# Eight dense layers on node features: a unit of two node chunks, one in each half of the partitions

## What is computed

```python
def _mlp1(x, W, b):
    return jax.nn.silu(x @ W + b)
def _res(h, W1, b1, W2, b2):
    return h + _mlp1(_mlp1(h, W1, b1), W2, b2)
res_h = nodes
h = _mlp1(nodes, Wh, bh)
h = _propagate(h, edge_attr, edge_index, We, be, Wl)
h = _res(h, r1_W1, r1_b1, r1_W2, r1_b2)
h = _mlp1(h, Wm, bm)
h = h + res_h
h = _res(h, r2_W1, r2_b1, r2_W2, r2_b2)
h = _res(h, r3_W1, r3_b1, r3_W2, r3_b2)
h = _propagate(h, edge_attr, edge_index, We, be, Wl)
```

## Time and profile before

| | us |
|---|---|
| median of 3 runs | 13832.53 |
| lowest and highest of them | 13831.42, 13838.11 |
| the profiled execution | 13845.22 |
| its span, first to last instruction | 13843.5 |

### The profile page before, as it was taken

How to read it: one execution, slowest core, us unless ns; L and a number is a source line. 1 busy time by engine, 2 the same in 40 slices (tenths; PEclk the granted TensorE clock), 3 DMA queues, 4 the chain that set the end, 5 groups by cost and what they waited for, 6 DMA issues and landing times.

```text
span 13843.5 us, 199525 instructions
## 1 busy us (share of the span) xinstructions
PE 9124.3 (66%) x43992; PEld 6407.8 (46%) x43993; DVE 7459.0 (54%) x18791; ACT 3827.0 (28%) x8556; POOL 9553.0 (69%) x8478
## 2 busy tenths in 40 slices
PE   0266665776663679897666666766666656667676
PEld 0011112222111345554666666466666655666666
DVE  8876665777761220101343333333343348999998
ACT  0144445444410111111222222222222222333332
POOL 0168887888886766564777777467777757777774
PEclk9999999999996779898555555555555555665665
DMA  9942222222226999799644444244444438999996
GB/s 380 406 90 19 20 19 14 20 20 20 20 14 216 379 354 324 278 325 219 110 106 104 103 103 104 54 97 104 104 105 104 104 82 171 178 177 177 177 179 128
DMA packets 1476698, 1975.29 MB, mean 143 GB/s; under 512 B 1005691, under 2 KB 1023803, under 8 KB 1410045
## 3 DMA queue, kind: packets, MB, share of 16 engines
q1 hardware_dynamic: 744700, 1265.08, 34.4%
q0 software_dynamic: 454160, 346.91, 14.8%
q10 hardware_dynamic: 277362, 357.67, 8.1%
HBM read 1466.26 MB, written 503.63 MB: 142 GB/s over the span
## 4 chain that ended last, share of the span: by engine, by line
POOL 41%; issue 20%; DMA 13%; PE 11%; SPq 7%; DVE 6%; ACT 1%; DVEq 1%; POOLq 0%; ACTq 0%
POOL gat L793 24%; POOL adj L745 14%; DMA b_row<-acc 5%; PE bank L1230 4%; DMA adj<-put_n,put_at 4%; POOL rec_src L731 4%; SPq L684 3%; DMA arena<-adj 2%; SPq L691 2%; DMA rec_src<-pay,ring_i 2%; DVE arena L1585 1%; PE same L1374 1%; PE bank L1118 1%; SPq L679 1%; PE same L1165 1%
## 5 line engine op out<-in xcount | busy, mean ns | idle before, releaser
L793 POOL DMA_INDIRECT gat<-q_table,ring_i x3456 | 3482.4, 1008 | 1368.9 <-issue 1051.5
L745 POOL DMA_INDIRECT adj<-put_n,put_at x1632 | 2558.5, 1568 | 1276.2 <-DVE put_at L1669 660.1
L1396 PE MATMUL bank<-onehot_t,onehot 128*128 128x64 f32 x6912 | 1585.0, 424 | 1424.8 <-DVE acc L1887 973.6
L731 POOL DMA_INDIRECT rec_src<-pay,ring_i x1632 | 1740.1, 1066 | 866.9 <-issue 491.3
L1396 PEld LDWEIGHTS bank<-onehot_t,onehot 128*128 128x128 f32 x6912 | 1507.1, 331 | 1501.7 <-DVE acc L1887 850.9
L793 POOL DMA_INDIRECT arena<-h_table,ring_i x1728 | 1753.6, 1015 | 629.4 <-issue 503.3
L1300 PE MATMUL same<-onehot 32*128 32x512 f16 x3264 | 1680.0, 616 | 620.7 <-DVE onehot L1640 392.8
L1648 DVE TENSOR_SCALAR_CACHE_REDUCE onehot<-same 128x128 bf16<-128x128 f32 (+3 forms) x1632 | 1232.6, 755 | 867.0 <-PE same L1302 816.4
L1386 PE MATMUL bank<-hs,arena 128*128 x6912 | 1565.3, 422 | 89.7 <-ACT arena L1020 89.6
L1386 PEld LDWEIGHTS bank<-hs,arena 128*128 128x128 f32 x6912 | 1525.9, 334 | 92.8 <-issue 92.8
L902 ACT ACTIVATE arena<-iota_lo,arena 128x128 bf16<-128x128 f32 x3264 | 995.8, 387 | 1109.3 <-PE bank L1125 1009.2
(11 more groups left out here) (321 smaller groups left out, 13965.8 us busy)
## 6 DMA issues: line engine op xcount, KB each, us to landing
arena<-adj SPq DMA_DIRECT2D x240, 1280.0 KB
arena<-rec_src SPq DMA_DIRECT2D x3456, 69.0 KB
adj<-hs ACTq DMA_DIRECT2D x25, 6656.0 KB, 46.4
arena<-adj SPq DMA_DIRECT2D x60, 2560.0 KB, 18.1
rec_src<-pay ACTq DMA_DIRECT2D x1, 119232.0 KB, 332.3
arena<-lo_row SPq DMA_DIRECT2D x3456, 32.0 KB
hs<-b_row SPq DMA_DIRECT2D x432, 256.0 KB
acc<-b_row SPq DMA_DIRECT2D x432, 256.0 KB
```

The costliest lines, as they stand in the source:

```text
L731: nc.gpsimd.indirect_dma_start(rec_src, bass.IndirectOffsetOnAxis(ring_i[:, q, u:u + 1], 0), pay[:, q, u, :], None, bounds_check=SLOTS - 1 ...
L745: nc.gpsimd.indirect_dma_start(counts, bass.IndirectOffsetOnAxis(put_at[:, b // 3 % 4, c:c + 1], 0), put_n[:, b // 3 % 4, c:c + 1], None, ...
L793: nc.gpsimd.indirect_dma_start(rows[n][:, u, :], None, table, bass.IndirectOffsetOnAxis(ring_i[:, n, u:u + 1], 0)).then_inc(landed[n], 16)
L1396: last = mm(bank[6 + n % 2][:, u // 2 * D:(u // 2 + 1) * D], onehot[:, n % 2, u, :], msg[n % 2][:, u, :], start=u % 2 == 0, stop=u % 2 == 1)
```

## The change

The feature arrays use all 128 partitions: even chunks lie in the lower half, odd chunks in the upper half, at the same columns (`feat`). A unit is such a pair; there are seven (`UNITS`), six of two full chunks and a last one with the single chunk of 128 nodes. The weights and biases of the eight layers and of the projection are loaded twice, once for each half. For each unit PE does two matmuls of 64 rows and 64 columns, one from the lower half of SBUF to the lower half of a bank and one from the upper to the upper, and signals once; ACT and DVE do one instruction of 128 partitions for each unit. Each unit waits for its own predecessor in the layer before, and banks 2 and 3 go on in turn across layers. To bring odd chunks into the upper half, the two transposing stages use plain matmuls against the identity (`spread=True`) in place of the transpose instruction. SP no longer waits for `f_res` before the edge loads of the second message passing.

```diff
+UNITS = -(-NCH // 2)
...
-        FT = [arena[0:D, n * NP:(n + 1) * NP] for n in range(3)]
+        FT = [arena[:, n * UNITS * CH * P:(n + 1) * UNITS * CH * P] for n in range(3)]
+        assert 3 * UNITS * CH * P <= 2 * NP
...
-        w_mlp = {m: sb(f"w_{m}", [D, D]) for m in MLPS}
-        b_mlp = {m: sb(f"b_{m}", [D, 1]) for m in MLPS}
-        w_pq = sb("w_pq", [D, 2 * D])
+        w_mlp = {m: sb(f"w_{m}", [2 * D, D]) for m in MLPS}
+        b_mlp = {m: sb(f"b_{m}", [2 * D, 1]) for m in MLPS}
+        w_pq = sb("w_pq", [2 * D, 2 * D])
+
+        def unit(t, u):
+
+            if u < UNITS - 1:
+                return t[:, u * CH * P:(u + 1) * CH * P]
+            return t[0:D, u * CH * P:u * CH * P + CHUNKS[-1][1] * P]
+
...
+        def of_chunk(t, c, at=0):
+
+            return halves(t, c % 2)[:, at:at + CHUNKS[c][1] * P]
+
+        def feat(t, c):
+
+            return of_chunk(t, c, c // 2 * CH * P)
+
+        def chunks_upto(u):
+
+            return min(2 * u + 2, NCH)
...
-        W_LOADS = 4 * len(CONVS) + 2 * len(MLPS) + 15
+        W_LOADS = 4 * len(CONVS) + 4 * len(MLPS) + 17
...
-                    sp.wait_ge(f_res, NCH * 4)
...
-                load(w_mlp[m][:], a["L2_gnn_" + wn])
-                load(b_mlp[m][:], a["L2_gnn_" + bn].rearrange("(d o) -> d o", o=1))
-            load(w_pq[:, 0:D], a["L2_gnn_We"][0:D, :])
-            load(w_pq[:, D:2 * D], a["L2_gnn_We"][D:2 * D, :])
+                for n in range(2):
+                    load(halves(w_mlp[m], n), a["L2_gnn_" + wn])
+                    load(halves(b_mlp[m], n), a["L2_gnn_" + bn].rearrange("(d o) -> d o", o=1))
+            for n in range(2):
+                load(halves(w_pq, n)[:, 0:D], a["L2_gnn_We"][0:D, :])
+                load(halves(w_pq, n)[:, D:2 * D], a["L2_gnn_We"][D:2 * D, :])
...
-                act.copy(FT[0][:, c0_ * P:(c0_ + n) * P], bank[c % 2][0:D, 0:n * P]).then_inc(n_cp, 1)
+                act.copy(feat(FT[0], c), of_chunk(bank[c % 2], c)).then_inc(n_cp, 1)
...
             def layer_act(j, m, dst):
-                for c, (c0_, n) in enumerate(CHUNKS):
-                    act.wait_ge(f_mm, NCH * j + c + 1)
-                    act.activation(dst[:, c0_ * P:(c0_ + n) * P], bank[2 + c % 2][0:D, 0:n * P], ACT.Silu,
-                                   bias=b_mlp[m][:, 0:1]).then_inc(f_act, 1)
+                for u in range(UNITS):
+                    rows = slice(0, 2 * D if u < UNITS - 1 else D)
+                    act.wait_ge(f_mm, UNITS * j + u + 1)
+                    act.activation(unit(dst, u), bank[2 + (UNITS * j + u) % 2][rows, 0:unit(dst, u).shape[1]], ACT.Silu,
+                                   bias=b_mlp[m][rows, 0:1]).then_inc(f_act, 1)
...
-            def transposes(tr, wait_h, src=h, width=D):
...
                     for j in range(n):
-                        last = nc.tensor.transpose(bank[c % 2][0:width, j * P:(j + 1) * P], src[:, c0_ + j, :], ident[:])
+                        if spread:
+                            last = mm(halves(bank[c % 2], c % 2)[:, j * P:(j + 1) * P], src[:, c0_ + j, :], ident[:], start=True, stop=True)
+                        else:
+                            last = nc.tensor.transpose(bank[c % 2][0:width, j * P:(j + 1) * P], src[:, c0_ + j, :], ident[:])
                     last.then_inc(n_tr, 1)
...
-            chunk = transposes(TR_L2, 3)
+            chunk = transposes(TR_L2, 3, spread=True)
...
             def layer_pe(j, m, src, ready, value):
-                pe.wait_ge(ready, value)
-                for c, (c0_, n) in enumerate(CHUNKS):
-                    if c >= 2:
-                        pe.wait_ge(f_act, NCH * j + c - 1)
-                    mm(bank[2 + c % 2][0:D, 0:n * P], w_mlp[m][:], src[:, c0_ * P:(c0_ + n) * P],
-                       start=True, stop=True).then_inc(f_mm, 1)
+                for u in range(UNITS):
+                    pe.wait_ge(ready, value(u))
+                    if UNITS * j + u >= 2:
+                        pe.wait_ge(f_act, UNITS * j + u - 1)
+                    for c in range(2 * u, chunks_upto(u)):
+                        last = mm(of_chunk(bank[2 + (UNITS * j + u) % 2], c), halves(w_mlp[m], c % 2), feat(src, c), start=True, stop=True)
+                    last.then_inc(f_mm, 1)
...
             def ft(c, j):
-                return FT[1][:, (c * CH + j) * P:(c * CH + j + 1) * P]
-
-            layer_pe(0, "h", FT[0], n_cp, NCH * (TR_L2 + 1))
-            pe.wait_ge(f_act, NCH)
-            project(EV_PQ, ft, w_pq[:], 2 * D)
+                return feat(FT[1], c)[:, j * P:(j + 1) * P]
+
+            copied = lambda tr: lambda u: NCH * tr + chunks_upto(u)
+            units = lambda j: lambda u: UNITS * j + u + 1
+            pq = lambda c: halves(w_pq, c % 2)
+
+            layer_pe(0, "h", FT[0], n_cp, copied(TR_L2))
+            pe.wait_ge(f_act, UNITS)
+            project(EV_PQ, ft, pq, 2 * D)
...
-            chunk = transposes(TR_MEAN, 4)
+            chunk = transposes(TR_MEAN, 4, spread=True)
...
-            layer_pe(1, "r1_1", FT[1], n_cp, NCH * (TR_MEAN + 1))
-            layer_pe(2, "r1_2", FT[2], f_act, NCH * 2)
-            layer_pe(3, "m", FT[1], f_res, NCH)
-            layer_pe(4, "r2_1", FT[1], f_res, NCH * 2)
-            layer_pe(5, "r2_2", FT[2], f_act, NCH * 5)
-            layer_pe(6, "r3_1", FT[1], f_res, NCH * 3)
-            layer_pe(7, "r3_2", FT[2], f_act, NCH * 7)
-            pe.wait_ge(f_res, NCH * 4)
-            project(EV_PQ + 1, ft, w_pq[:], 2 * D)
+            layer_pe(1, "r1_1", FT[1], n_cp, copied(TR_MEAN))
+            layer_pe(2, "r1_2", FT[2], f_act, units(1))
+            layer_pe(3, "m", FT[1], f_res, units(0))
+            layer_pe(4, "r2_1", FT[1], f_res, units(1))
+            layer_pe(5, "r2_2", FT[2], f_act, units(4))
+            layer_pe(6, "r3_1", FT[1], f_res, units(2))
+            layer_pe(7, "r3_2", FT[2], f_act, units(6))
+            pe.wait_ge(f_res, UNITS * 4)
+            project(EV_PQ + 1, ft, pq, 2 * D)
             for c, (c0_, n) in enumerate(CHUNKS):
                 if c >= 2:
                     pe.wait_ge(n_cp, NCH * TR_BACK + c - 1)
                 for j in range(n):
-                    last = nc.tensor.transpose(bank[c % 2][:, j * D:(j + 1) * D], ft(c, j), ident[0:D, 0:D])
+                    o = c % 2 * D
+                    last = nc.tensor.transpose(bank[c % 2][:, j * D:(j + 1) * D], ft(c, j), ident[o:o + D, o:o + D])
...
             def residual(j, n, other):
-                for c, (c0_, m) in enumerate(CHUNKS):
-                    dve.wait_ge(f_act, NCH * j + c + 1)
-                    cols = slice(c0_ * P, (c0_ + m) * P)
-                    v.tensor_tensor(FT[1][:, cols], FT[1][:, cols], other[:, cols], ALU.add).then_inc(f_res, 1)
+                for u in range(UNITS):
+                    dve.wait_ge(f_act, UNITS * j + u + 1)
+                    v.tensor_tensor(unit(FT[1], u), unit(FT[1], u), unit(other, u), ALU.add).then_inc(f_res, 1)
...
-                cols = slice(c0_ * P, (c0_ + n) * P)
-                v.tensor_tensor(FT[1][:, cols], FT[1][:, cols], bank[c % 2][0:D, 0:n * P], ALU.add).then_inc(n_cp, 1)
+                v.tensor_tensor(feat(FT[1], c), feat(FT[1], c), of_chunk(bank[c % 2], c), ALU.add).then_inc(n_cp, 1)
```

More of the change, by code:

```diff
@@ L1134, in hist_end, with transposes @@
                 mm(bank[6][:, 0:NH], zero_bf[:, 0:P], zero_bf[:, 0:NH], start=False, stop=True).then_inc(p_hist_end, 1)
-            def transposes(tr, wait_h, src=h, width=D):
+            def transposes(tr, wait_h, src=h, width=D, spread=False):
                 def chunk(c):
```

## The result

The changed kernel takes 13724.3 us (median of 4 runs, 13719.7 to 13727.4) beside 13835.3 for the kernel before on the same chip (4 runs, 13831.4 to 13841.3): ratio 0.9921, with a 95% interval from 0.9906 to 0.9937. That is -111 us, where -104 was forecast, and 13724.3 lies in the forecast's own range. The profiled execution took 13723.2 us, with a span of 13721.5.

What follows compares the result with a forecast made beforehand. POOL leads the chain, but the dense stages lie on it alone, bound inside layers by PE at half clock. Start +2.5, layer 0 -9.8, projections -4.3 each, layers -88.1 sum to -104: 13832.5 becomes 13728.5, range 13714 to 13740.

Steps and rivals of the forecast that it cites:

- What bounds the kernel: Whole kernel: POOL carries 41% of the chain, PE 11%; dense layers and projections lie on it with nothing beside them.
- Layers 1 to 7: Layers at full clock: a bank's round of 2.26 us for two units bounds; 7.64 us a layer, 54.2 for seven.
- O1 can start with E2: Unit's records E1, E2 (even chunk), O1, O2 (odd): O1 runs beside E2, two steps of 0.43 us a unit on PE.
- The clock: PE in the layers: full clock throughout, since borders lose their wait and two streams run; otherwise falls after layer 1.
- Two row halves on one bank: Layers' pairs: taken to overlap as the rows suggest, 13728; by the skill's rule they could not, 13755 to 13838.
- The transposes: Both transposing stages get slower: 98 records for 49, round 1.83 us; layer 1 starts at 8873.0, not 8870.6.
- Layer 0: First projection's start moves from 6536.8 to 6527.0, table load 2.6 us later included: -9.8 us.
- The projections: Both projections: 22.1 us each unchanged at half clock, 13.5 at full clock (-8.6); half taken, -4.3 each.
- The start: 18 more loads on ACT's queue delay blanking and fill 11.7 us; POOL's early batches wait longer: +2.5 us, 0 if covered.
- half the clock: Rival in the layers: pairs overlap but the clock falls as before, 12.5 us a layer, 13768 us; chance 0.13.
- the serial pair of 10.8 us a layer: Rival in the layers: pairs run one after the other at full clock, 1.71 us a unit, 13755.5 us; chance 0.11.
- a drain at each change of tile: Rival in layers and transposes: serial, half clock, each tile change waits 0.19 us, some 120 times, 13861 us; chance 0.05.

Runs made afterwards that it cites:

- number 5: Changed kernel with SP's wait on f_res put back into the loads of the edges: 13720.0 us, ratio 0.9932 to the kernel before.
- number 3: Changed kernel with the 18 added loads moved behind the blanking DMAs on ACT's queue: 13766.0 us, ratio 0.9926 to the kernel before.
- number 10: Changed kernel with odd chunks reading the even chunk's features and weights, pairs apart in columns alone, output wrong: 13741.3 us, ratio 0.9942 to the kernel before.
- number 4: Changed kernel with four PSUM banks for the layers in place of two: 13752.9 us, ratio 0.9913 to the kernel before.
- number 1: Changed kernel with both halves, but each layer waits until the layer before is complete: 13761.7 us, ratio 0.9924 to the kernel before.
- 3 to 9: Also covers: changed kernel with two-block transposes, 13722.7 us; that plus paired projections and four layer banks, 13686.6 us; the same kernel again, 13686.7 us.
- 11: Changed kernel with two-block transposes, paired projections and four layer banks, plus ACT copying half of the projections' evacuation: 13676.2 us, ratio 0.9905 to the kernel before.
- number 2: Kernel before, 64 partitions, each chunk waiting only for its own predecessor and banks in turn across layers: 13860.1 us, ratio 0.9992.
- number 12: Kernel before with only the 18 further loads of weights, into partitions that nothing reads: 13823.3 us, ratio 1.0005.
- number 7: Changed kernel with the projection alternating between the blocks of two chunks, each chunk in its own bank: 13696.2 us, ratio 0.9916 to the kernel before.

## Why the prediction was right, and where not

**What bounds the kernel** held: the dense stages were on the chain with nothing beside them, and what was taken from them came out of the total nearly one for one (-108.6 by stages, -111 by medians; -96 in number 5 and -100 in number 3, kernels with the same dense stages, on two other chips). That the total came within 7 us of the forecast is in part luck: 6.5 us too few in the layers, and a spread of 15 us between chips. The low end of the forecast's range has a slip as well: both projections at the full clock and the start for nothing give 13717, not 13714.

**Layers 1 to 7: mechanism right, size off by 6.5 us.** The prediction said "In program order O1 can start with E2", so that a unit lasts three steps until it has drained. That O2 starts two steps behind E1 is the term that was mis-sized. In the profile E1 and O1 start together (in number 10 too, where they share their rows), O2 is one step behind, and so the round is shorter: 0.43 + 0.59 + 0.69 and 0.24 for the handovers, 1.95 us against 2.26. A layer is three rounds and 0.86, 6.7 us against 7.64, and seven take 47.7 against 54.2. That the round of a bank is the bound was right: number 4 takes it away and the layers fall to 39.3.

**The clock: right, for a reason that was half right.** Two streams in different rows and columns kept it: all ten profiles of such kernels (the changed one, numbers 1 and 3 to 9, and 11) have 1.00 through all seven layers, and the three profiles of single matmuls (before, numbers 2 and 12) lose it in layer 2. Two streams as such are not enough: number 10 lost it in layer 6. What the clock goes by isn't shown beyond these cases. That nothing breaks the work any more did not matter: with the borders back (number 1) it stayed, and with single matmuls and borders no longer than the changed kernel's (number 2) it fell. The prediction put the fall "behind the border to layer 2"; it did stand there, but the border isn't what decides.

**Two row halves on one bank.** The E and O matmuls of a unit are different row tiles, write one bank at the same time, and overlap completely: two records of 611 and 640 ns that start at 8850.4, and in number 4 a unit of four records each 0.86 us. They write different partitions of that bank. By the Trainium skill, page "TensorEngine Tiling (Array Packing)", section "Gotcha 1: PSUM Pressure", they could not; the trace decides against it for this case. Different row halves that write the same partitions of one bank at once weren't tried, since nothing orders such a pair; number 7 runs them in different banks.

**The transposes** took 12.7 us, 0.8 more than worked out. The third chunk waited for DVE and began at 8833.7, still at half the clock, which rose at 8834.4, 3.5 us into them, and a round took 1.86 us for 1.83; by these rows that is some 0.4 us, and the other half stays open.

**Layer 0** was -10.4 for -9.8, with the table load 2.6 us later against the transposes, as forecast. Number 12 shows that some 7.8 us of it depend on when the clock fell in the execution that was profiled: beside that execution, with 20.3 us for the same stretch, the gain is 2.3 us. So the agreement of -10.4 with -9.8 is in part the choice of profile.

**The projections: the sum right by accident.** "At the half clock nothing changes" was wrong, and -4.3 was a mean of two cases neither of which came. The clock was 0.50 in 17.2 of 18.8 us, and yet 95 records took 17.20 us, 0.181 each, where before 96 took 20.86, 0.217 each. Even and odd chunks now read different rows, and a chunk begins beside the one before it, as soon as its own bank is empty: two chunks in 3.04 us instead of 3.41. DVE in the changed kernel, the first of its two copies for three chunks in a row:

```profile
8895.68 0.42 DVE L1872 COPY hs<-same 128x256 f32<-128x256 f32 x1 [1.16 <-PE same L1190]
...
8896.70 0.42 DVE L1872 COPY hs<-same 128x256 f32<-128x256 f32 x1
...
8898.72 0.42 DVE L1872 COPY hs<-same 128x256 f32<-128x256 f32 x1 [1.14 <-PE same L1190]
```

The second chunk is ready 1.02 us behind the first, though eight matmuls at half the clock need 1.7: the last four of one chunk run beside the first four of the next. What bounds a pair is then the round of its bank, 2.07 us of PE, 0.88 of DVE and 0.09 for the handovers. Number 7, where every neighbour is such a pair, gives 11.2 us and confirms the overlap.

**The start** was right in size, +2.7 for +2.5, with the blanking beginning at 45.0 us for 33.2, and number 12 puts it down to the loads but for number 1's profile. The way there was another: not long landings for some 12 us more, but 3.1 us gained at the first addition, 4.0 lost in the eighth batch and 2.2 at the sixteenth landing, at 923 us, where the last of the long landings ended at 766. That these add up to the forecast is luck. **SP's wait** was worth nothing (number 5).

**The rivals.** No stretch of the layers shows half the clock, the serial pair of 10.8 us a layer, or a drain at each change of tile.

## What to carry to other kernels

If a matmul has 64 rows and 64 columns, put a second, independent one beside it that reads and writes the other half of the partitions: here a step was 0.43 us for one record and for two, and ACT's and DVE's instructions on 128 partitions cost what 64 did (0.687 us for 0.682, 0.692 for 0.684). After that read the evacuation: here the round of two banks, then DVE's two copies, were the bound, and more banks gave another 8.4 us in the layers and pairs another 7.5 a projection; the Trainium skill, page "TensorEngine Tiling (Array Packing)", section "PSUM Bottleneck", says of a fourfold faster TensorE that the copy out of PSUM may become the bottleneck and that both engines should share it, and numbers 4, 7 and 11 agree with it here, at twice the rate. When a clock falls near a wait, don't take the wait for the cause before an experiment has removed it.

## What the runs showed of the hardware that was not expected

- Single 64-row, 64-column float32 matmuls, with PE busy 14.00 of 14.50 us, lost the full clock in layer 2 (number 2; so did the kernel before and number 12); two at a time in different rows and columns kept it for 58.0 us in the changed kernel, with PE idle for 0.46 us at each border. Two at a time in the same 64 rows ran as fast and lost it at 8892.4, 44.4 us after it had risen.
- Two at a time that share their rows and write different halves of a bank started together (8863.6) and ran at 6.70 us a layer, as did those apart in both.
- Matmuls of 64 rows and 128 columns in different row halves and different banks overlap completely: 32 in 2.06 us, and 98 in 7.2 us of busy time.
- ACT's copy of 256 float32 columns out of PSUM took 0.33 us, DVE's 0.41.
